# Two transformer layers on eight cores: the DMAs of the expert weights' preparation move from GpSimd's queue to SP's

## The chip, the cores and the metric

One Trainium2 chip, all 8 cores. Each core computes one of the 8 batch elements (2048 tokens of 1024 features), with no exchange between cores. The metric is the device time in microseconds of the slowest core.

## The reference

Layer 0 normalises x, and adds to x an attention (16 heads of 64, K also used as V) and a mixture of 8 experts. Layer 1 normalises again, and adds a causal attention with rotary embedding and a linear layer with ternary weights. The change lies in the experts of layer 0. Every expert is computed for every token; the two best by the router are weighted and summed:

```
g = softmax(h @ Wr); top2_w, top2_idx = top_k(g, 2); top2_w /= sum(top2_w)
hid = relu(einsum('bsh,ehf->bsef', h, W1))          # W1: 8 x 1024 x 4096
expert_out = einsum('bsef,efh->bseh', hid, W2)      # W2: 8 x 4096 x 1024
out = sum(take(expert_out, top2_idx) * top2_w)
```

## The kernel before

The kernel is written for five queues (TensorE, VectorE, ScalarE, GpSimd, SP). A small helper, `PB`, appends each operation to the list of its engine in the order of the Python code, and derives waits from the names (keys) that an operation reads and writes. An engine works through its list strictly in that order: an instruction that waits holds all behind it. `fence()` makes every key that is written for the first time afterwards wait for all semaphores as they stand at the fence, except for keys named as exempt.

The stages stand in this order in the code: `ln0`, `attn0`, `moe0`, `ln1`, `attn1`, `ffn1`.

`emit_attn0` loads its weights through the tile `stg` (two slots of 128 x 1024 fp32) with SP's queue and casts on VectorE. It ends with a fence that exempts `stg0`, `stg1`, `castb0` and `castb1`.

`emit_moe0` then has three parts.

1. SP loads `selb`, `idf32` and `wrstg`. The router runs over 16 tiles of 128 tokens (TensorE, VectorE, ScalarE).
2. The preparation (the loop at L686 to L730) turns the expert weights from fp32 into bf16 and lays them out for the loop, through scratch tensors `sw1` and `sw2` in HBM. For each of 8 experts it has 32 units for W1 and 32 for W2, 512 in all. A unit loads 512 KB into a slot of `stg`, casts it on GpSimd into a slot of `castb`, and stores 256 KB to `sw1` or `sw2`. A W1 load has contiguous runs of 2 KB, a W2 load of 512 B. Slots alternate. The store has `serialize=True`, so it also waits for the store before it on the same semaphore, two units earlier. All eight experts are written out here, ahead of part 3.
3. The expert loop goes over 8 experts and 4 blocks of 512 tokens, 32 passes. In a pass SP loads 8 blocks of 1 MB from `sw1` into `w1buf` (two slots; L755 multiplies, L763 applies ReLU into `hid`) and 8 blocks from `sw2` into `w2buf` (two slots; L776 multiplies, L784 and L788 weight and add to x). These loads read the keys `pp{ex}` and `ppB{ex}`, the last stores of that expert's preparation. A pass begins with the VectorE copy `cbs` (L740).

The helper's DMAs all carry L110 in the profile, or L134 where SP's waits are listed.

The lines that the change touches have this form, six of them:

```
pb.dma("gpsimd", stg[slot] <- w1_d[ex] ..., "pga"/"pgb", writes=[stg slot])
pb.op("gpsimd", castb[slot] <- stg[slot], reads=[stg slot], writes=[castb slot])
pb.dma("gpsimd", sw1_d[ex, fg] ... <- castb[slot], "ppw"/"ppw2", reads=[castb slot], serialize=True)
```

Of the kernel before, what the change touches and what calls it, by code (L numbers as in the profile page):

```python
# [150 lines left out]
def build_nc(stages=ALL_STAGES, dbg=None):  # L151
# [29 lines left out]
    with ExitStack() as ctx:  # L181
        pb = PB(nc, ctx)
# [424 lines left out]
        def emit_moe0(xn_done):  # L607
# [81 lines left out]
            for ex in range(NEXP):  # L689
                for fg in range(8):  # L690
                    for q in range(4):
                        slot = pti % 2
                        pti += 1
                        pb.dma("gpsimd",
                               stg[:, slot * 1024:(slot + 1) * 1024].rearrange(
                                   "p (c f) -> p c f", f=NT),
                               w1_d[ex].rearrange("(c p) (g f) -> g p c f",
                                                  p=128, f=NT)[fg][:, q * 2:(q + 1) * 2, :],
                               "pga" if slot == 0 else "pgb",
                               writes=[f"stg{slot}"])  # L700
                        pb.op("gpsimd", lambda e, slot=slot: e.tensor_copy(  # L701
                            castb[:, slot * 1024:(slot + 1) * 1024],
                            stg[:, slot * 1024:(slot + 1) * 1024]),
                            reads=[f"stg{slot}"], writes=[f"castb{slot}"])
                        pb.dma("gpsimd",
                               sw1_d[ex, fg, :, q * 1024:(q + 1) * 1024],
                               castb[:, slot * 1024:(slot + 1) * 1024],
                               "ppw" if slot == 0 else "ppw2",
                               reads=[f"castb{slot}"], serialize=True)
                for dc in range(8):  # L710
                    for qt in range(4):
                        slot = pti % 2
                        pti += 1
                        pb.dma("gpsimd",
                               stg[:, slot * 1024:(slot + 1) * 1024].rearrange(
                                   "p (fc j) -> p fc j", j=128),
                               w2_d[ex].rearrange("(fc p) (c j) -> c p fc j",
                                                  p=128, j=128)[dc][:, qt * 8:(qt + 1) * 8, :],
                               "pga" if slot == 0 else "pgb",
                               writes=[f"stg{slot}"])  # L720
                        pb.op("gpsimd", lambda e, slot=slot: e.tensor_copy(  # L721
                            castb[:, slot * 1024:(slot + 1) * 1024],
                            stg[:, slot * 1024:(slot + 1) * 1024]),
                            reads=[f"stg{slot}"], writes=[f"castb{slot}"])
                        pb.dma("gpsimd",
                               sw2_d[ex, dc, :, qt * 1024:(qt + 1) * 1024],
                               castb[:, slot * 1024:(slot + 1) * 1024],
                               "ppw" if slot == 0 else "ppw2",
                               reads=[f"castb{slot}"], serialize=True)
                pb._dep_update((), [f"pp{ex}"], ("ppw", pb.cnt["ppw"]))  # L730
                pb._dep_update((), [f"ppB{ex}"], ("ppw2", pb.cnt["ppw2"]))
# [540 lines left out]
        if "moe0" in stages:  # L1272
            emit_moe0(xn_done)
# [91 lines left out]
```

How the kernel before makes its waits and increments, by code:

```python
            def body(eng):  # L131
                for w, fn, incs in ops:
                    for s, c in w:
                        eng.wait_ge(sems[s], c)
                    ins = fn(eng)
                    for s, n in incs:
                        ins.then_inc(sems[s], n)
```

## Time and profile before

| | |
|---|---|
| median of the runs | 7590.35 us (7580.98 to 7599.72, 2 runs) |
| profiled execution | 6954.24 us, span of the slowest core 6952.5 us |
| spans of the eight cores | 6910.1 to 6952.5 us |
| mean granted TensorE clock | 0.878 to 0.881 |
| bytes moved by DMA, slowest core | 989.70 MB |

The profiled execution is shorter than the runs shown. Its rows are used for durations, and the sum of the prediction is made against its own time. A row of a group of instructions gives the line, the engine, the operation, output and input, and the count; "idle before" is how long the engine stood still just ahead of them, and what ended that. A row on DMA issues gives the median time from issue to landing. SPq is SP's queue.

### The profile page before, as it was taken

What the parts mean: (1) busy time and instruction counts of PE and PEld (TensorE: products, weight loads), DVE (VectorE), ACT (ScalarE), POOL (GpSimd) and SP (SyncE); (2) the same over time, 40 slices, a digit from 0 to 9 for tenths busy, and PEclk for the clock granted to TensorE, in tenths of its full rate; (3) what the DMA queues carried; (4) which work ended last, traced back from release to release, by engine and by line L of the source; (5) the groups of instructions that cost most, each with busy time, mean ns of one, the idle gap of its engine ahead of it and who ended that gap; (6) DMA issues with size and microseconds to landing.
All of it is one profiled execution on the core that took longest, in us unless ns stands there. A gap on an engine that the chain in (4) does not pass through costs nothing.

```text
span 6952.5 us, 84185 instructions; the slowest of 8 cores (6910.1 to 6952.5 us)
## 1 busy us (share of the span) xinstructions
PE 5330.6 (77%) x23271; PEld 2135.9 (31%) x23271; DVE 1426.1 (21%) x2644; ACT 1930.5 (28%) x2829; POOL 1247.7 (18%) x1553
## 2 busy tenths in 40 slices
PE   3666666656999999999999999999999335555536
PEld 0222222212444444444444444444444011111102
DVE  5222222222101010101010101001101633333336
ACT  0355555541111111111212111111111025545531
POOL 0233333332222222222222222220000000000000
PEclk9877777877999999999999999999999566767768
DMA  2434333335777777777777777775444000000011
GB/s 60 126 106 104 110 105 109 114 114 173 214 223 221 230 226 222 222 224 226 222 223 221 216 226 223 223 227 167 151 148 151 0 22 4 4 7 3 4 52 70
DMA packets 209081, 989.70 MB, mean 142 GB/s; under 512 B 27110, under 2 KB 37486, under 8 KB 141050
## 3 DMA queue, kind: packets, MB, share of 16 engines
q1 hardware_dynamic: 92794, 573.21, 25.3%
q0 software_dynamic: 115840, 411.11, 20.9%
q8 instruction: 210, 3.44, 0.2%
q14 instruction: 237, 1.94, 0.1%
HBM read 841.61 MB, written 142.61 MB: 142 GB/s over the span
## 4 chain that ended last, share of the span: by engine, by line
PE 57%; DMA 15%; ACT 11%; DVE 10%; issue 6%; DVEq 0%; ACTq 0%; SPq 0%; POOL 0%; POOLq 0%
PE bankA L776 20%; PE bankA L755 20%; DMA w1buf<-sw 7%; ACT exp L360 7%; DMA w2buf<-sw 6%; PE bankB L350 5%; PE bankA L338 2%; PE bank L493 2%; ACT rtmpB L927 1%; PE bankA L1132 1%; PE bankA L1233 1%; DVE rhl L450 1%; DVE rb L1083 1%; DVE rb L460 1%; DVE t1s L289 1%
## 5 line engine op out<-in xcount | busy, mean ns | idle before, releaser
L776 PE MATMUL bankA<-hid,w2buf 128*128 128x512 bf16 x8192 | 1793.0, 380 | 93.0 <-DMA w2buf<-sw 63.6
L755 PE MATMUL bankA<-xnTs,w1buf 128*128 128x512 bf16 x8192 | 1798.0, 381 | 69.7 <-DMA w1buf<-sw 69.2
L763 ACT ACTIVATE hid<-bankA 128x512 bf16<-128x512 f32 x1024 | 611.8, 598 | 3094.7 <-PE bankA L755 3094.7
L776 PEld LDWEIGHTS bankA<-hid,w2buf 128*128 128x128 bf16 x8192 | 794.8, 98 | 1091.3 <-issue 156.6
L755 PEld LDWEIGHTS bankA<-xnTs,w1buf 128*128 128x128 bf16 x8192 | 795.2, 98 | 1064.2 <-issue 133.1
L360 ACT ACTIVATE exp<-bankA,colpool 128x1024 bf16<-128x1024 f32 x832 | 908.1, 1114 | 493.9 <-PE bankA L338 459.6
L784 DVE TENSOR_TENSOR mtmp<-bankA,cbs 128x512 f32<-128x512 f32 x256 | 177.1, 692 | 3350.7 <-PE bankA L776 3350.7
L721 POOL CAST castb<-stg 128x1024 bf16<-128x1024 f32 x256 | 270.8, 1058 | 1502.0 <-DMA stg<-l0w 1502.0
L701 POOL CAST castb<-stg 128x1024 bf16<-128x1024 f32 x256 | 271.0, 1059 | 1488.4 <-DMA stg<-l0w 1488.4
L110 POOL DMA_DIRECT2D stg<-l0w x512 | 419.2, 819 | 229.8 <-DVE wkbf L310 204.4
L350 PE MATMUL bankB<-exp,vG 128*65 128x512 bf16 x640 | 258.8, 467 | 132.6 <-DVE exp L371 76.0
L110 POOL DMA_DIRECT2D sw<-castb x512 | 284.2, 555 | 279.0 <-POOL castb L721 139.6
L110 POOL DMA_DIRECT2D outT<-xTs x8 | 4.2, 536 | 1365.9 <-DVE xTs L1143 1365.6
L448 DVE CAST rhl<-rrow 1x512 bf16<-1x512 f32 x64 | 28.9, 451 | 882.4 <-ACT rrow L445 882.4
L788 DVE TENSOR_TENSOR xTs<-xTs,mtmp 128x512 f32<-128x512 f32 x256 | 188.0, 734 | 27.6 <-DVE mtmp L784 1.4
L452 PE MATMUL bankA<-rhl,onesb 1*128 1x512 bf16 x64 | 33.7, 527 | 181.6 <-DVE rhl L448 181.6
L371 DVE TENSOR_TENSOR exp<-exp,cmaskS 128x512 bf16<-128x512 bf16 x256 | 97.4, 422 | 337.7 <-ACT exp L360 337.7
L350 PE MATMUL bankB<-exp,vA0b 128*65 128x512 bf16 x256 | 110.7, 432 | 58.6 <-ACT exp L360 53.3
L350 PE MATMUL bankB<-exp,vA0a 128*65 128x512 bf16 x256 | 109.4, 427 | 58.6 <-ACT exp L360 53.3
L1075 PE MATMUL bank<-rhl,onesb 1*128 1x512 bf16 x64 | 35.7, 558 | 152.4 <-DVE rhl L1071 152.4
L338 PE MATMUL bankA<-qT,kT 64*128 64x512 bf16 x640 | 150.1, 465 | 0.1
L350 PEld LDWEIGHTS bankB<-exp,vG 128*65 128x65 bf16 x640 | 61.2, 119 | 282.2 <-issue 282.2
(218 smaller groups left out, 3167.4 us busy)
## 6 DMA issues: line engine op xcount, KB each, us to landing
stg<-l0w POOLq DMA_DIRECT2D x512, 512.0 KB, 5.7
w1buf<-sw SPq DMA_DIRECT2D x256, 1024.0 KB, 7.3
w2buf<-sw SPq DMA_DIRECT2D x256, 1024.0 KB, 7.1
sw<-castb POOLq DMA_DIRECT2D x512, 256.0 KB, 3.9
xTs<-xT SPq DMA_DIRECT2D x8, 1024.0 KB, 17.2
wtf<-l1wt SPq DMA_DIRECT2D x16, 512.0 KB
outT<-xTs POOLq DMA_DIRECT2D x8, 1024.0 KB, 11.6
stg<-l0wq SPq DMA_DIRECT2D x8, 512.0 KB, 4.5
```

The source lines that it names most:

```text
L110: self.on(qeng, lambda e, o=out, i=in_: e.dma_start(o, i), wait=w, inc=[(sem, 16)])
L338: lambda e, kc=kc, h12=h12, q4=q4, t=t: e.matmul(bank[q4][:, :], t["klhsT"](kc, h12), t["qrhs"][h12], start=True, stop=True),
L350: lambda e, kp=kp, h12=h12, q4=q4, t=t, nkc=nkc: e.matmul(bank[4 + h12][0:65, :], t["vap"](kp, h12), t["expb"][:, q4 * NT:(q4 + 1) * NT], ...
L360: lambda e, pp=pp, t=t: e.activation(t["expb"][:, pp * NT:(pp + 2) * NT], bankA[:, pp * NT:(pp + 2) * NT], AF.Exp, bias=t["negcol"]),
L493: e.matmul(bnk[:, :], wbf[:, dc * 1024 + hp * 128: dc * 1024 + (hp + 1) * 128], xnch(dc)[:, t0:t0 + NT], start=(dc == 0), stop=False),
L701: pb.op("gpsimd", lambda e, slot=slot: e.tensor_copy(castb[:, slot * 1024:(slot + 1) * 1024], stg[:, slot * 1024:(slot + 1) * 1024]), read ...
L721: pb.op("gpsimd", lambda e, slot=slot: e.tensor_copy(castb[:, slot * 1024:(slot + 1) * 1024], stg[:, slot * 1024:(slot + 1) * 1024]), read ...
L755: e.matmul(bnk[:, :], w1buf[:, slot * 4096 + dc * NT + fp * 128: slot * 4096 + dc * NT + (fp + 1) * 128], xnch(dc)[:, t0:t0 + NT], start=( ...
L763: pb.op("scalar", lambda e, f=f, bnk=bnk: e.activation(hid[:, f * NT:(f + 1) * NT], bnk[:, :], AF.Relu), reads=[bkkey], writes=[f"hid{f % ...
L776: e.matmul(bnk[:, :], w2buf[:, slot * 4096 + fc * 128:slot * 4096 + (fc + 1) * 128], hid[:, fc * NT:(fc + 1) * NT], start=(fc == 0), stop= ...
L784: pb.op("vector", lambda e, bnk=bnk, mslot=mslot: e.tensor_tensor(mtmp[:, mslot * NT:(mslot + 1) * NT], bnk[:, :], cbs[:], ALU.mult), read ...
L788: pb.op("vector", lambda e, dc=dc, t0=t0, mslot=mslot: e.tensor_tensor(xch(dc)[:, t0:t0 + NT], xch(dc)[:, t0:t0 + NT], mtmp[:, mslot * NT: ...
```

## The change

The queue of four DMA calls in the preparation is changed from `gpsimd` to `sync` (SP): the load and the store of the W1 units, and the load and the store of the W2 units. The casts, the tiles, the semaphores, their values, and the order of the code stay as they are. No function is new.

```
@@ preparation of W1, per unit @@
-                        pb.dma("gpsimd",
+                        pb.dma("sync",
                                stg[:, slot * 1024:(slot + 1) * 1024] ... <- w1_d[ex] ...
...
-                        pb.dma("gpsimd",
+                        pb.dma("sync",
                                sw1_d[ex, fg, :, q * 1024:(q + 1) * 1024],
                                castb[:, slot * 1024:(slot + 1) * 1024],
@@ preparation of W2, per unit @@
-                        pb.dma("gpsimd",
+                        pb.dma("sync",
                                stg[:, slot * 1024:(slot + 1) * 1024] ... <- w2_d[ex] ...
...
-                        pb.dma("gpsimd",
+                        pb.dma("sync",
                                sw2_d[ex, dc, :, qt * 1024:(qt + 1) * 1024],
                                castb[:, slot * 1024:(slot + 1) * 1024],
```

## Rows read from the trace of the kernel before

**Rows 1.** The page: busy time, share of the span and instructions of each engine.

```profile
PE 5330.6 (77%) x23271; PEld 2135.9 (31%) x23271; DVE 1426.1 (21%) x2644; ACT 1930.5 (28%) x2829; POOL 1247.7 (18%) x1553
```

**Rows 2.** Windows of core 0: length, busy us, granted clock, DMA share, GB/s.

```profile
2200.00:4600.00 2400.00, 2283.65 (x10407) 1007.78 (x10405) 246.50 (x348) 382.44 (x640) 593.45 (x738) 1.00 0.73 224
4800.00:5395.00 595.00, 589.42 (x2722) 265.31 (x2720) 64.92 (x96) 95.59 (x160) 0.00 (x0) 1.00 0.41 149
```

**Rows 3.** Tiles stg and sw, whole span: duration ns min/median/max, first and last start.

```profile
L110 POOL DMA_DIRECT2D stg<-l0w x512: 722/882/1133, 205.1 to 4729.1; - x171
...
L110 POOL DMA_DIRECT2D sw<-castb x512: 552/557/569, 211.0 to 4740.2; - x171
```

**Rows 4.** Waits of SP's queue: us in total, times, longest.

```profile
SPq L134 <- PE bankA L456: 1328.6, 1, 1328.6
...
SPq L134 <- DVE wqbf L315: 6.1, 8, 0.8
```

**Rows 5.** Timeline, 1527 to 1553 us: start, us, engine, line, operation.

```profile
1533.46 1.04 POOL L721 CAST castb<-stg 128x1024 bf16<-128x1024 f32 x1 [4.16 <-DMA stg<-l0w]
...
1535.05 0.55 POOL L110 DMA_DIRECT2D sw<-castb  x1 [0.54 <-POOL castb L721]
...
1542.64 0.69 DVE L471 TENSOR_TENSOR xTs<-xTs,t1s 64x512 f32<-64x512 f32 x1
...
1543.99 0.27 SPq L110 DMA_DIRECT2D selb<-sel  x1
1550.15 0.36 SPq L110 DMA_DIRECT2D idf<-idf32c  x1
...
1552.26 0.40 SPq L110 DMA_DIRECT2D wrstg<-l0wr  x1
...
1552.82 1.05 SPq L110 DMA_DIRECT2D w1buf<-sw  x2
```

**Rows 6.** DMA issues (KB, median us to landing); tiles stg; w1buf after 5100.

```profile
w1buf<-sw SPq DMA_DIRECT2D x256, 1024.0 KB, 7.3
w2buf<-sw SPq DMA_DIRECT2D x256, 1024.0 KB, 7.1
...
stg<-l0wq SPq DMA_DIRECT2D x8, 512.0 KB, 4.5
stg<-l0wk SPq DMA_DIRECT2D x8, 512.0 KB, 4.4
stg<-l1wq SPq DMA_DIRECT2D x8, 512.0 KB, 3.7
stg<-l1wo SPq DMA_DIRECT2D x8, 512.0 KB, 4.1
...
L110 SPq DMA_DIRECT2D stg<-l0wq x8: 327/328/426, 163.0 to 180.5; - x8
L315 DVE TENSOR_SCALAR wqbf<-stg x8: 693/694/695, 167.8 to 185.1; 128x1024 bf16<-128x1024 f32 x8
...
DMA to landing us min/median/max: 4.7/4.9/10.4
```

**Rows 7.** Preparation beside attention, W1 units 205 to 440 us, W2 units 440 to 672.

```profile
L110 POOL DMA_DIRECT2D stg<-l0w x33: 722/722/913, 205.1 to 434.6; - x33
L701 POOL CAST castb<-stg x32: 1030/1035/2272, 209.4 to 432.5; 128x1024 bf16<-128x1024 f32 x32
...
DMA to landing us min/median/max: 4.2/4.6/6.0
DMA to landing us min/median/max: 3.2/3.4/4.8
...
L110 POOL DMA_DIRECT2D stg<-l0w x30: 911/911/942, 442.3 to 668.5; - x30
...
DMA to landing us min/median/max: 4.8/5.4/6.2
DMA to landing us min/median/max: 2.9/3.7/5.0
```

**Rows 8.** Timeline of VectorE: first, later passes, and the expert loop's last addition.

```profile
1633.43 0.69 DVE L740 COPY cbs<-bankB 128x512 f32<-128x512 f32 x1 [1.97 <-PE bankB L736]
...
4719.07 0.69 DVE L740 COPY cbs<-bankB 128x512 f32<-128x512 f32 x1
4835.32 0.69 DVE L740 COPY cbs<-bankB 128x512 f32<-128x512 f32 x1
...
5284.19 0.68 DVE L740 COPY cbs<-bankB 128x512 f32<-128x512 f32 x1
...
5395.57 0.69 DVE L788 TENSOR_TENSOR xTs<-xTs,mtmp 128x512 f32<-128x512 f32 x1
```

More of the change, by code:

```diff
@@ L693, in emit_moe0 @@
                         pti += 1
-                        pb.dma("gpsimd",
+                        pb.dma("sync",
                                stg[:, slot * 1024:(slot + 1) * 1024].rearrange(
@@ L704, in emit_moe0 @@
                             reads=[f"stg{slot}"], writes=[f"castb{slot}"])
-                        pb.dma("gpsimd",
+                        pb.dma("sync",
                                sw1_d[ex, fg, :, q * 1024:(q + 1) * 1024],
@@ L713, in emit_moe0 @@
                         pti += 1
-                        pb.dma("gpsimd",
+                        pb.dma("sync",
                                stg[:, slot * 1024:(slot + 1) * 1024].rearrange(
@@ L724, in emit_moe0 @@
                             reads=[f"stg{slot}"], writes=[f"castb{slot}"])
-                        pb.dma("gpsimd",
+                        pb.dma("sync",
                                sw2_d[ex, dc, :, qt * 1024:(qt + 1) * 1024],
```

## The prediction

> **What bounds the kernel now.** I read the shares of the span first [rows 1], then the busy time by stretch [rows 2], then what each queue waited for [rows 3, 4], then single transfers in order of time [rows 5 to 7], and last the step of the expert loop [rows 8].
>
> The span has four stretches. Layer norm and loading of the attention weights run to 205 us. Attention of layer 0 follows; the last write of its result starts at 1542.64 and lasts 0.69 us, so it ends at 1543.3 [rows 5]. After the router, the experts run from 1633.4 to 5395.6, the start of their last addition [rows 8]. What comes behind takes 1557 us up to the span's end of 6952.5. In the experts TensorE is busy for 2283.65 us of 2400 (95%) at granted clock 1.00 while weights are also being prepared, and for 589.42 us of 595 (99%) once that is over [rows 2]. So TensorE bounds the expert stretch, and a small part is waiting for weights.
>
> The preparation is a second chain, wholly on GpSimd's queue: 512 units, each a load of 512 KB, a cast, and a store of 256 KB. It runs from 205.1 to 4740.2 plus the last store [rows 3], which is (4740.2 - 205.1)/512 = 8.86 us a unit. It is strictly serial, since a load is queued behind the store before it, and that store behind its cast. Today almost nobody waits for it: it has (1543 - 205)/7.2 = 186 units, nearly three experts' work, behind it when attention ends. The reader should see that GpSimd's busy share is only 18% [rows 1], and that this chain is all the same 4535 us long. It is hidden because it lies beside attention and beside the experts.
>
> **The change, part by part.** Three edits move all 1024 DMAs of the preparation (512 loads, 512 stores) from GpSimd's queue to SP's. The 512 casts stay on GpSimd. What counts is where they come to stand in SP's order. SP's queue at that point holds, in order: `selb`, `idf32` and `wrstg`, then (new) all 1024 DMAs for all eight experts, and then the 512 loads of `w1buf` and `w2buf` of the expert loop.
>
> *Ahead of them.* The load of `selb` is the first use of a new key behind the fence of the attention, so it waits for the attention's end. The trace has this as one wait of SP of 1328.6 us [rows 4], and the load goes at 1543.99 [rows 5]. On GpSimd's queue the preparation did not pass this fence (its keys are exempt) and started at 205.1. On SP's it stands behind `selb` and starts where the first `w1buf` load starts now, 1552.8 [rows 5]. The whole overlap with attention is gone.
>
> *Behind them.* The loads of `w1buf` for expert 0 need only the preparation of expert 0, but they are queued behind the preparation of expert 7. So TensorE, after the router (which ends near 1633 as now, and hides under the preparation), has nothing to do until all 512 units are through. The overlap with the experts is gone too. The preparation, at nothing today, now costs all it takes. Who waits behind: SP's loads, then TensorE on `w1buf`, then ScalarE and VectorE on TensorE, and layer 1 on them.
>
> *The unit on SP.* Its order stays serial: load, landing, cast, store issue, next load. The store does wait for the store two units before, which has long landed (median 3.4 to 3.7 us [rows 7]), and costs nothing.
> - Load, issue to landing. On SP no load of this preparation exists in the trace. Nearest are 512 KB loads of the same size into the same tile: `l1wq`, whose runs of 512 B have the shape of the w2 half, lands after 3.7 us, with nothing in front of it; `l0wq` and `l0wk` take 4.5 and 4.4 with the next load beside them, `l1wo` 4.1 [rows 6]. From GpSimd's queue, with the unit's own store just in front, it is 4.6 for w1 and 5.4 for w2 in the attention stretch, 0.72 and 0.91 of it the issue [rows 7], where SP's issue is 0.33 [rows 6]. Taking the difference in issue off gives 4.2 and 4.8. I take 4.5 for both; ends 3.7 and 5.2.
> - Cast 1.04 [rows 7].
> - Hops: SP waits 6.1 us in 8 times for casts by VectorE that last 0.69 [rows 4, 6], 0.76 each time, so a hop is below 0.1. Two hops and four waits for SP to work through: 0.2.
> - Store issue 0.33, as other loads and stores of 128 rows on SP [rows 6], and a gap of 0.04. On GpSimd this was 0.54 of idleness and 0.56 of issue behind each cast [rows 5, 7], so SP's path is some 0.7 us shorter.
>
> Sum 4.5 + 1.04 + 0.2 + 0.37 = 6.1 us. The ends are 3.7 + 1.61 = 5.3, and 7.2, which is GpSimd's own pace beside attention, (434.6 - 205.1)/32 [rows 7]. 8.86, its mean over everything, held only while 1 MB loads of the expert loop ran in the same engines; in the changed kernel they do not overlap at all, so I leave 8.86 to a rival.
>
> At this place the Trainium skill, page "DMA: Bandwidth & Descriptors", section "Specifications", gives about 1 us to the first byte from GpSimd's path and 0.6 from the hardware path. By it the unit would be 0.8 us shorter for its two transfers than GpSimd's 7.2, that is 6.4, and the preparation 154 us longer than by my value. The trace has no first byte to compare with.
>
> *What comes back.* Without the preparation's traffic, the loads of the expert loop land after 4.9 us instead of 7.3 and 7.1 [rows 6]. One pass (expert and 512 tokens) now takes (4719.07 - 1633.43)/26 = 118.7 us, and after the preparation's end (5284.19 - 4835.32)/4 = 112.2 [rows 8]. All 32 passes run at the second pace: 3590 us, where the stretch takes 3762 now. Gain 172 us. Attention loses its neighbour on the DMA engines; no row shows it waiting for a DMA, so nothing. If that is wrong it is a few tens of microseconds.
>
> **Sum, for the profiled execution.** 1552.8 (start of the preparation) + 512 x 6.1 = 3123 + 5 (first `w1buf` landing) + 3590 + 1557 (tail) = 9828 us, against 6954 now: +2874.
>
> The runs shown have a median of 7590, 636 above the profiled execution; no row shows where these lie. If they are a fixed amount, the changed kernel gets 636 as well; if a share of the time (9.15%), 900. A slower TensorE step in those runs would partly hide in the loop's waits for weights before and could not after, so I go between, 770. Predicted: 9828 + 770 = 10,600 us, some 40% slower.
>
> **Rivals.**
> - *The unit keeps its mean pace of 8.86.* For it: same bytes, same engines, and small runs of 512 B in the w2 half. Against it: beside attention it was 7.2, and the rise came only with the loop's loads. It would give 1552.8 + 4536 + 5 + 3590 + 1557 + 770 = 12,010.
> - *Loads run ahead.* The two slots of `stg` would allow a pace like that of the `l0wq` loads, (180.5 - 163.0)/7 = 2.5 us a load [rows 6], or about 3.8 with the stores' bytes: 9828 - 512 x 2.3 + 770 = 9420. Against it: the store of a unit stands ahead of the next load in SP's order and waits for the cast; it would need the order of a queue to be broken.
> - *The other side: no stall in front.* If the fence did not hold SP, and the loop's loads did not stand behind all the units, only the shorter unit would be left (8.86 less 1.1, as 7.2 becomes 6.1). The preparation would end near 205 + 512 x 7.8 = 4200 and the loop would gain at most the 172 us: 7590 - 172 = 7420, faster by 2.3%. The place is SP's queue at the first `w1buf` load, and the point from which it decides is whether that load goes near 1553 or after the last unit. Against it: the order in the code, and the wait of 1328.6 us [rows 4].
> - *Nothing to see.* Moving a DMA from one queue to another changes only its issue, 0.82 us and 0.56 us of GpSimd's time that nobody waits for: 7590. Against it: the same two reasons. The Trainium skill has this rule, "DMA: Bandwidth & Descriptors", section "Issuing engines are not separate DMA queues": where a DMA is issued saves only the sequencer's time. It speaks of bandwidth, and I follow it there (my landing times barely differ by queue); it says nothing of order.
>
> **How the numbers follow.** Forecast (unit between 5.3 and 7.2) 0.88; unit at 8.86 or near it 0.06; loads ahead 0.04; the other side 0.01; nothing to see 0.01. Every case but the last two is slower by far more than 2%, which is about what a measurement of this kernel can tell from no change: slower 0.98, same 0.01, faster 0.01. The range comes from the unit and the carrying over to the runs: low 9828 - 512 x 0.8 + 640 = 10,060; high 9828 + 512 x 1.1 + 900 = 11,290. The cases outside are the tails.
>
> **What would show it.** The first preparation load at about 1550 instead of 205. TensorE idle, and the DMA engines at about 768 KB in 6.1 us (some 130 GB/s), from about 1640 to 4680. GpSimd's casts 6.1 us apart, w1 and w2 halves nearly alike. The first `w1buf` load right behind the last store. Passes of 112 us, no waits for weights. Attention and layer 1 as long as now. I am wrong in kind if `w1buf` is loaded before the last unit or the preparation begins before 1540, and wrong in size mainly by the unit: 0.1 us in it is 51 us in the end.

## The result, and the profile after

The changed kernel is slower: 1.4186 times the kernel before (95% interval 1.4126 to 1.4245). It takes 9903 to 9915 us, its profiled execution 9914.8. The two runs of 7581 and 7600 us shown ahead of the prediction were disturbed ones; of the ten runs that the kernel before has by now, the five undisturbed ones took 6953 to 7022, near its profiled execution of 6954.

In microseconds this lies below the range of the prediction (10,060 to 11,290); the section on why the prediction was right, and where it was off, says which step put it there.

The page of the kernel before, busy tenths in 40 slices of its span:

```profile
PE   3666666656999999999999999999999335555536
...
POOL 0233333332222222222222222220000000000000
...
DMA  2434333335777777777777777775444000000011
```

The page of the changed kernel, shares of the span and the 40 slices (compare [rows 1]):

```profile
span 9912.7 us, 85699 instructions; the slowest of 8 cores (9841.1 to 9912.7 us)
...
PE 5305.8 (54%) x23271; PEld 2143.3 (22%) x23271; DVE 1404.8 (14%) x2644; ACT 1929.9 (19%) x2829; POOL 539.5 (5%) x529
...
PE   3766661000000000000799999999999998355554
...
POOL 0000001111111111111000000000000000000000
...
DMA  2000003444444444444444444444444442000002
```

TensorE's busy time is what it was, 5306 against 5331 us. What is new is a hole of twelve slices in its row, and GpSimd, which was busy from slice 2 to slice 27, is now busy in that hole and just ahead of it. In the attention, slices 2 to 6, the DMA engines now do nothing. This is the whole change at one look: a chain that lay beside two stages now stands between them.

The mean granted clock of TensorE fell from 0.878 to 0.755 on the slowest cores, which could look like a cause. It is not one: in the hole TensorE has no work, and in the expert loop it has the full clock, as before [rows 2]. Windows of core 7 (length, busy us of PE, PEld, DVE, ACT and POOL, granted clock, DMA share, GB/s):

```profile
1700.00:4700.00 3000.00, 0.00 (x0) 0.00 (x0) 0.00 (x0) 0.00 (x0) 497.64 (x479) 0.50 0.45 126
4800.00:8300.00 3500.00, 3467.64 (x16002) 1558.44 (x16000) 361.95 (x527) 599.97 (x1004) 0.00 (x0) 1.00 0.42 151
```

SP's queue around the fence, and around the end of the preparation (timeline: start, us, engine; compare [rows 5]):

```profile
1541.06 0.27 SPq L110 DMA_DIRECT2D selb<-sel  x1
1542.93 0.36 SPq L110 DMA_DIRECT2D idf<-idf32c  x1
1545.16 0.40 SPq L110 DMA_DIRECT2D wrstg<-l0wr  x1
1545.61 0.57 SPq L110 DMA_DIRECT2D stg<-l0w  x1
...
4745.92 0.37 SPq L110 DMA_DIRECT2D stg<-l0w  x1
4751.49 1.04 POOL L721 CAST castb<-stg 128x1024 bf16<-128x1024 f32 x1 [6.11 <-DMA stg<-l0w]
4752.62 0.34 SPq L110 DMA_DIRECT2D sw<-castb  x1
4753.01 0.91 SPq L110 DMA_DIRECT2D w1buf<-sw  x2
4761.28 4.00 PE L755 MATMUL bankA<-xnTs,w1buf 128*128 128x512 bf16 x9 [3135.28 <-DMA w1buf<-sw]
```

The first unit starts 0.45 us behind `wrstg`, the first load of `w1buf` 0.39 us behind the last store, and TensorE has waited 3135.28 us for it. The wait is put down to a DMA, but that DMA landed 8.1 us after it was issued at 4753.01. It was issued late, and the row that tells so is SP's.

What SP's queue waited for (us in total, times, longest; compare [rows 4]), and the DMA issues (KB, median us to landing; compare [rows 6]):

```profile
SPq L134 <- POOL castb L721: 1370.8, 256, 6.8
SPq L134 <- POOL castb L701: 1337.4, 256, 6.2
SPq L134 <- PE bankA L456: 1327.6, 1, 1327.6
...
stg<-l0w SPq DMA_DIRECT2D x512, 512.0 KB, 4.4
w1buf<-sw SPq DMA_DIRECT2D x256, 1024.0 KB, 4.9
w2buf<-sw SPq DMA_DIRECT2D x256, 1024.0 KB, 4.9
sw<-castb SPq DMA_DIRECT2D x512, 256.0 KB, 3.4
```

The one wait of 1327.6 us is the old one; it used to cost nothing. The 512 waits for casts, 2708 us, are new. SP waits there for the unit's own load and cast, and everything behind them in the queue waits too.

### The profile page after: what moved, and what is told of

It reads as the page before. It is cut to its first block, busy times and chain, and to the rows that moved or that the text cites. A ratio compares the mean times of both kernels' runs of the same rounds, so it can differ in the third digit from the quotient of the medians.

```text
span 9912.7 us, 85699 instructions; the slowest of 8 cores (9841.1 to 9912.7 us)
## 1 busy us (share of the span) xinstructions
PE 5305.8 (54%) x23271; PEld 2143.3 (22%) x23271; DVE 1404.8 (14%) x2644; ACT 1929.9 (19%) x2829; POOL 539.5 (5%) x529
## 2 busy tenths in 40 slices
DMA packets 504004, 989.78 MB, mean 100 GB/s; under 512 B 27110, under 2 KB 299630, under 8 KB 435962
## 4 chain that ended last, share of the span: by engine, by line
PE 46%; DMA 25%; ACT 7%; DVE 7%; POOL 5%; issue 5%; SPq 2%; POOLq 0%; DVEq 0%; ACTq 0%
DMA stg<-l0w 23%; PE bankA L755 17%; PE bankA L776 17%; ACT exp L360 4%; PE bankB L350 3%; POOL castb L701 3%; POOL castb L721 3%; SPq L110 2%; PE bankA L338 2%; PE bank L493 1%; ACT rtmpB L927 1%; PE bankA L1132 1%; PE bankA L1233 1%; DMA w1buf<-sw 1%; DVE rb L1083 0%
## 5 line engine op out<-in xcount | busy, mean ns | idle before, releaser
L755 PE MATMUL bankA<-xnTs,w1buf 128*128 128x512 bf16 x8192 | 1777.5, 379 | 3137.0 <-DMA w1buf<-sw 3137.0
L350 PE MATMUL bankB<-exp,vB0a 128*65 128x512 bf16 x256 | 111.0, 434 | 14.0 <-DVE t1s L467 14.0
L350 PE MATMUL bankB<-exp,vB0b 128*65 128x512 bf16 x256 | 108.2, 423 | 14.4 <-DVE t1s L467 14.4
```

The source lines that it names most:

```text
L350: lambda e, kp=kp, h12=h12, q4=q4, t=t, nkc=nkc: e.matmul(bank[4 + h12][0:65, :], t["vap"](kp, h12), t["expb"][:, q4 * NT:(q4 + 1) * NT], ...
L755: e.matmul(bnk[:, :], w1buf[:, slot * 4096 + dc * NT + fp * 128: slot * 4096 + dc * NT + (fp + 1) * 128], xnch(dc)[:, t0:t0 + NT], start=( ...
```

## The experiments

The theory: the transfers are as fast on SP as they were, and the loss is made of order alone. (1) The fence ahead of the preparation takes away the attention as a cover. (2) The expert loop's loads behind all 512 units take away the loop as a cover. (3) The store between a cast and the next load keeps the unit serial. Rivals: SP's queue or its transfers are slow in themselves, the DMA engines are the bound, or the loss grows with the number of DMAs moved. Every experiment computes the whole result. e1 to e5 have one profiled execution and no interval; they are compared by it, and the differences at stake are hundreds of us.

### e1: only the loads on SP

```
-                        pb.dma("gpsimd", stg[slot] <- w1_d / w2_d ...
+                        pb.dma("sync",   stg[slot] <- w1_d / w2_d ...
                         pb.dma("gpsimd", sw1_d / sw2_d <- castb[slot] ...     (as before)
```

> Change only half made: the 512 loads go on SP, the 512 stores stay on GpSimd. Theory (SP works strictly in order, and in the changed kernel each store stood between a cast and the next load): SP still starts behind the attention (first load near 1546 us) and the expert loop's loads still stand behind all 512 loads, but loads now run one unit ahead, so a unit takes 3.0 to 3.6 us; 1546 + 512 x 3.3 + 5 + 3593 + 1558 = 8390 us. Rival (a unit's time is the transfers' own, whatever the order): the unit stays at 6.3 us and the time at 9910.

Measured: 8662.6 us. The first load goes at 1531.7 us, behind the fence. The units take (3511.7 - 1531.7)/512 = 3.87 us, above the 3.0 to 3.6 that were forecast, so the time of 8390 was too short. The loop's first load goes at 3502.6, behind the last load of the preparation.

The timeline of GpSimd in this kernel tells the missing 0.57 us:

```profile
2001.54 1.04 POOL L721 CAST castb<-stg 128x1024 bf16<-128x1024 f32 x1 [1.05 <-DMA stg<-l0w]
...
2003.12 0.54 POOL L110 DMA_DIRECT2D sw<-castb  x1 [0.54 <-POOL castb L721]
2006.18 1.04 POOL L721 CAST castb<-stg 128x1024 bf16<-128x1024 f32 x1 [2.52 <-DMA sw<-castb]
```

The loads do run ahead, and now it is the cast that waits for a slot of `castb`, whose store of two units before lands only after a median of 5.7 us here. What ended the idle time ahead of the casts (us in total, times):

```profile
  DMA sw<-castb: 829.2, 354
```

With that, theory (3) holds: taking the stores out of SP's order makes a unit 2.4 us shorter, with the same bytes. The rival of a fixed unit falls. The forecast of the unit was too short because a second pair of slots became the limit.

### e2: only the stores on SP

```
                         pb.dma("gpsimd", stg[slot] <- w1_d / w2_d ...         (as before)
-                        pb.dma("gpsimd", sw1_d / sw2_d <- castb[slot] ...
+                        pb.dma("sync",   sw1_d / sw2_d <- castb[slot] ...
```

> The other half: loads and casts on GpSimd, stores on SP. Theory: GpSimd prepares two units near 205 us and then waits for slots of castb, because the first store stands behind the fence in SP's queue (about 1546 us). The loop's loads stand behind all stores. A unit is 0.72 to 0.91 issue, landing 4.6 to 5.4 with the issue, cast 1.04 and some 0.5 before the next issue: 6.6 us. 1546 + 510 x 6.6 + 5 + 3593 + 1558 = 10070 us, the slowest of all although half of the DMAs did not move. Rival (the loss grows with the number of DMAs that are moved to SP): half the loss, about 8430.

Measured: 9983.88 us (forecast 10,070), even slower than the full change. GpSimd's timeline shows the fence at work through another engine:

```profile
213.60 1.03 POOL L701 CAST castb<-stg 128x1024 bf16<-128x1024 f32 x1 [3.41 <-DMA stg<-l0w]
214.58 0.73 POOL L110 DMA_DIRECT2D stg<-l0w  x1
1532.71 1.03 POOL L701 CAST castb<-stg 128x1024 bf16<-128x1024 f32 x1 [1317.41 <-DMA sw<-castb]
```

Two units are cast, the third waits 1317.41 us for a store that stands in SP's queue behind `selb`. From there a unit takes (4827.9 - 1528.7)/510 = 6.47 us, where 6.6 was forecast. Half of the DMAs moved cost all of the loss, so it is not their number that counts.

### e3: the preparation written ahead of the fence

```
+            (the whole preparation loop, all on "sync")
             pb.dma("sync", selb[:, :], sel_d[:, :], "dmisc", writes=["selb"])
...
-            (the preparation loop, behind the router)
```

> The changed kernel with one move in the order of the code: the whole preparation is written ahead of the load of selb, so on SP it no longer stands behind the attention's end; the loop's loads (and the router's) still stand behind all 512 units. Theory: first unit near 205 us, 6.3 us a unit, end near 3430; then the three small loads and the router, 85 us, and the loop at 112 us a pass: 3430 + 85 + 3593 + 1558 = 8670 us. So the fence is worth about 1250 us of the loss of 2950 and the loop's loads behind the last unit the rest. Rival (the fence is harmless, the queue is slow in itself): no change from 9910.

Measured: 8795 and 8802 us on cores 2 and 3, at granted clocks of 0.782 and 0.784, and 8578 to 8651 on the other six, at 0.788 to 0.801; the forecast was 8670. I read core 5, the shortest, 8578.1; the same core took 9865.3 in the changed kernel and 6921.5 in the kernel before. Its rows (duration, first and last start), tiles `stg` and `cbs`:

```profile
L110 SPq DMA_DIRECT2D stg<-l0w x512: 378/379/1888, 207.6 to 3344.9; - x171
...
L740 DVE COPY cbs<-bankB x32: 681/684/690, 3431.3 to 6907.1; 128x512 f32<-128x512 f32 x32
```

On this core the preparation starts at 207.6 instead of 1526.2, and its last load goes 1338 us earlier (3344.9 instead of 4682.6). The time falls by only 1287, mainly because the router is no longer hidden: from the last load to the loop's first matmul it is 86 us instead of 13. A pass is (6907.1 - 3431.3)/31 = 112.1 us. Taking the fence away thus gives back 1287 of a loss of 2944 on this core, and 1261 to 1294 on each of the six cores. The remainder is the loop behind the last unit.

### e4: the loop's loads leave SP

```
-                        pb.dma("sync", w1buf[...] / w2buf[...] ...
+                        block_load(j + 2): pb.dma("scalar", w1buf[...] / w2buf[...] ...
                         (written behind the last matmul group of block j, whose slot it refills)
```

> The changed kernel with the expert loop's 512 loads of w1buf and w2buf issued from ScalarE's queue, each at the point of the order where its slot comes free; the preparation stays wholly on SP behind the fence. Theory: the loop no longer stands behind the preparation of all experts but behind that of its own. First pass at 1546 + 64 x 6.3 = 1950. From there the preparation, with the loop's traffic beside it, takes 7 to 8.3 us a unit, 64 units 450 to 530 us against 4 passes of 118 = 472: the two run about level. End of the preparation near 1950 + 448 x 7.6 = 5350, then the last expert, 449, and the tail 1558: 7360 us (7100 to 7600). Rival (moving the preparation to SP makes the transfers themselves slow, or the DMA engines are the bound): stays above 9000.

Measured: 7677.99 us, above the range of 7100 to 7600, and 2237 us less than the changed kernel. The loop's first matmul starts at 1935.4. Its waits for weights (us in total, times, longest):

```profile
PE bankA L767 <- DMA w1buf<-sw: 796.0, 72, 328.1
...
PE bankA L786 <- DMA w2buf<-sw: 73.5, 69, 3.0
```

The 328.1 is the wait for the first expert. Most of the rest falls at the changes of expert: a pass there takes 2596.65 - 2410.65 = 186 us against 117 within an expert. The preparation beside the loop took (5659.0 - 1925.7)/448 = 8.33 us a unit, 533 us an expert, from the last store of expert 0 to that of expert 7, and four passes of the loop need only some 470; I had reckoned with 7.6. So the loop follows the preparation throughout. The fence is untouched here, and the serial unit too; what was taken away is the place of the loop's loads behind all 512 units.

The gains of e3 and e4 do not add up to the loss: 1287 and 2237 are 3524, and the loss is 2960. Each was measured with the other stall in place. Once the loop waits only for its own expert, the fence costs it 64 units and not 512: its first matmul starts at 1935.4, some 300 us later than in the kernel before.

### e5: the stores one unit later in SP's order

```
-            load(i); cast(i); store(i)
+            load(i); cast(i); store(i - 1)
```

> The changed kernel with all DMAs on SP and the preparation at the same place, but each unit's store written behind the next unit's load (load i, store i-1), so that SP never holds a load back for a cast. Theory: first load near 1540 us, the unit goes from 6.26 to about 3.4 us (in the half change with stores on GpSimd it was 3.87, where the next cast waited for a store of 5.7 us; SP's stores land in 3.4), total 1540 + 512 x 3.4 + 9 + 3593 + 1558 = 8440 us (8340 to 8690). Rival (the transfers of one queue do not overlap usefully): 9900.

Measured: 8530.65 us in its profiled execution, within the 8340 to 8690 that were forecast. A unit takes (3377.5 - 1529.7)/512 = 3.61 us. All DMAs are on SP and the fence and the loop's place are as in the changed kernel; only the order inside the preparation differs, and 1384 us are gone. The median landing of a load is 5.3 us and of a store 3.9, both longer than in the serial unit (4.4 and 3.4); here a load and a store are under way together. The core moved 218 GB/s between 1700 and 3300 us, where the changed kernel moved 126 in its hole, so the DMA engines were not what bound the serial preparation.

### e6: nothing left behind the preparation

```
             (e3 and e4 together)
-            pb.dma("sync",   selb / idf32 / wrstg ...
+            pb.dma("scalar", selb / idf32 / wrstg ...
```

> The changed kernel with both stalls taken away and the serial unit kept: the preparation written ahead of the fence (as in e3), and the router's three loads and the expert loop's loads issued from ScalarE's queue (as in e4). Theory: nothing stands behind the preparation any more; it starts near 205 us, has 212 units behind it when the attention ends, and the remaining 300 at 8.3 us end near 4030, always ahead of the loop. Attention, router, loop and tail as in the kernel before, with 21 instead of 27 passes at 118.7 us and the rest at 112.2: 6915 us against 6953 before (6880 to 6990), so the queue itself costs nothing. Rival (part of the loss is in the hardware queue's transfers or in their contention with the loop): above 7200.

Measured: 0.9938 (0.9912 to 0.9965) of the kernel before, profiled execution 6903.73 us. All 1024 DMAs of the preparation are on SP in the serial form of the changed kernel. The loop runs from 1629.1.

```profile
L110 SPq DMA_DIRECT2D stg<-l0w x512: 378/384/2148, 206.7 to 4066.4; - x171
```

The last unit's load goes at 4066.4 (forecast 4030). In the same surroundings, attention and then loop, GpSimd's queue took from 205.1 to 4729.1 for the same loads [rows 3]. So the whole loss is gone, and SP's queue is not slow in itself: it is through 660 us sooner.

### e8: the control for e4 and e6

```
             (the kernel before; only the loop's loads as in e4)
```

> Control: the kernel before with only the expert loop's loads issued from ScalarE's queue, the preparation on GpSimd. Theory: the queue of the loop's loads is worth nothing, 6953 us within 0.5%. If it comes out slower, that amount is in e4 and e6 too and has to be taken off there.

Measured: 1.0024 (0.9977 to 1.0072). Whether SP or ScalarE issues the loop's loads is worth nothing that these runs can tell. The last load of its preparation, on GpSimd, goes at 4708.3, against 4066.4 in e6.

### e7, e10 and e11: all on SP, in the order of need

```
+            for i in range(384): unit_step(i)          # load(i), store(i-1); ahead of selb. 336 in e10, e11
             pb.dma("sync", selb ...
...
             pb.dma("sync", w1buf / w2buf ...            # block k of the loop
+            unit_step(384 + k)                          # while there are units left
```

> All DMAs on SP as in the changed kernel, put in the order in which they are needed: units pipelined (load i, store i-1), the first 384 written ahead of the fence, the last 128 one beside each block of the expert loop's first 8 passes. Theory: 384 units at 3.4 us fill the attention stretch (205 + 1310 = 1515); the loop starts near 1630; 8 passes with traffic beside them at about 120, 24 at 112.2; tail 1558: 1630 + 960 + 2693 + 1558 = 6840 us, against 6953 before (faster by 1.0 to 2.0%). If a unit in attention takes 3.9 us, the loop starts some 160 us later and the time is about 7000. Rival (any preparation on SP costs the loop): above 7100.

Measured: 0.9949 (0.9917 to 0.998), half a per cent faster, where 1 to 2% had been expected. In SP's timeline of this kernel the three small loads came too late:

```profile
1668.91 0.30 SPq L110 DMA_DIRECT2D selb<-sel  x1
1670.93 0.35 SPq L110 DMA_DIRECT2D idf<-idf32c  x1
1672.83 0.38 SPq L110 DMA_DIRECT2D wrstg<-l0wr  x1
1673.55 0.33 SPq L110 DMA_DIRECT2D w1buf<-sw  x1
```

A unit beside the attention took (1668.9 - 206.9)/384 = 3.8 us instead of 3.4, the units ahead of the fence overran the attention, and the router started some 125 us late. That is the stall of the changed kernel in small.

> As e7, with 336 units ahead of the fence instead of 384. In e7 a unit beside attention took 3.75 us and the loop started 125 us late. Theory: 336 x 3.75 = 1260, so the units ahead end near 1465, before the attention does, and the loop starts near 1630 as in the kernel before; 11 passes at 118, 21 at 112.2, tail 1558: 1630 + 1298 + 2356 + 1558 = 6842 us, and no more than 6870: some 1.3 to 1.8% under the kernel before (e7: 0.5%). Rival (e7's late start was not what it lost, but the clock or the DMA engines): no better than e7, 6900 or more.

Measured: 6849.13 us in its profiled execution (forecast 6842), without an interval; e11 is the same kernel. The last store ahead of the fence and what follows:

```profile
1399.90 0.37 SPq L110 DMA_DIRECT2D stg<-l0w  x1
1402.61 0.34 SPq L110 DMA_DIRECT2D sw<-castb  x1
1544.75 0.30 SPq L110 DMA_DIRECT2D selb<-sel  x1
...
1549.41 0.38 SPq L110 DMA_DIRECT2D stg<-l0w  x1
1549.94 3.01 SPq L110 DMA_DIRECT2D sw<-castb  x1
1553.01 1.40 SPq L110 DMA_DIRECT2D w1buf<-sw  x1
```

SP now waits for the attention's end with all due work done. The loop starts at 1631.2; its first 11 passes take (2933.81 - 1631.2)/11 = 118.4 us, later ones 112.0.

> The kernel of e10 once more, because only two of its eight runs were undisturbed and so its comparison had no interval. Theory as there: 6842 us, 0.980 to 0.986 of the kernel before. Rival: those two runs were lucky, 0.99 or above.

Measured: 0.9846 (0.9812 to 0.9879). This is the fastest version. Its gain over the kernel before is the passes without traffic beside them: 21 of 32, where it was 5.

## Why the prediction was right, and where it was off

In direction, mechanism and size of the loss it was right: the sum for the profiled execution was 9828 us, 2874 more than before, and the span is 9912.7, 2960 more. In the time that it named, 10,600 us, it was not: the runs took 9903 to 9915, below the low end of its range. By its own terms:

| term | predicted | measured |
|---|---|---|
| first unit | 1552.8 | 1545.6 |
| 512 units | 3123 (6.10 each) | 3207 (6.26 each) |
| to the first matmul | 5 | 8.7 |
| 32 passes | 3590 (112.2) | 3593 (112.2) |
| tail | 1557 | 1558 |

**The place in SP's order.** Right, and shown from both sides: e3 takes the fence away, e4 the loop's place, e6 both. The rivals "the other side" and "nothing to see" would have needed a preparation that starts near 205 us; its first load went at 1545.61. e6 is what the first of them would have looked like. It gave 0.9938, where 7420/7590 = 0.978 was worked out: that took the full 172 us of the loop, but some 21 passes still had the traffic beside them.

**The unit.** 6.26 instead of 6.10, 84 us in all. The transfer was right: over the 512 units the mean from a load's issue to its landing is 4.46 us, where 4.5 was put. The terms that were too small are the small ones. From the landing to the start of the cast it is 0.24, where a hop of 0.1 was put; from the store's issue to the next load's 0.44, where 0.37 was. The cast's end to the store's issue is 0.08. The hop of 0.1 had been read from SP waiting for VectorE; GpSimd waiting for a DMA is another wait, and none of the rows showed it. W1 units took (1742.0 - 1550.4)/31 = 6.18, W2 units (1946.4 - 1748.6)/31 = 6.38: alike, as forecast. Loads of the changed kernel from 1700 to 3200 us, and the timeline of two casts:

```profile
DMA to landing us min/median/max: 3.7/4.4/6.0
...
1556.92 1.04 POOL L701 CAST castb<-stg 128x1024 bf16<-128x1024 f32 x1 [5.47 <-DMA stg<-l0w]
1562.86 1.04 POOL L701 CAST castb<-stg 128x1024 bf16<-128x1024 f32 x1 [4.89 <-DMA stg<-l0w]
```

The estimate that followed from the Trainium skill, page "DMA: Bandwidth & Descriptors", section "Specifications", was 6.4, and my own 6.1; the measured 6.26 lies halfway, and does not decide between them.

**The first matmul.** 8.7 us instead of 5. The first two loads of `w1buf`, of 1 MB each, go 0.47 us apart and right behind the last store, and the first lands after 8.1 us, not after the median of 4.9.

**The rival of 8.86 us a unit.** Rightly set aside for the changed kernel, where nothing runs beside the preparation. But it shows what the loop's traffic does to a unit: e4, with the same order in the unit and the loop beside it, came to 8.33.

**What comes back.** Passes of 112.2 us, median landing of the loop's loads 4.9 us: right. The gain of 172 us is there; without it the loss would have been larger still.

**Attention and layer 1.** As long as before: the attention's end moved by 3 us, the tail by 1.

**The carrying over to the runs.** This step failed. I added 770 us, between a fixed amount and a share, since the median shown lay 636 us above the profiled execution. The changed kernel's time is level with its profiled execution, and so is that of the kernel before. The right amount was 0, and the right sentence would have been 9828. The 636 us belonged to those two runs, not to the kernel, and no row of the trace spoke for them. Even the low end of the range had 640 us of it, so the time came out below the range. That the ratio is near all the same, 10,600/7590 = 1.397 against 1.4186, is luck: the 770 above the line and the 636 below it nearly cancel. The profiled sums alone give 9828/6954 = 1.413, inside the interval.

**A slip.** The prediction speaks of three edits; the diff has four, and the counts of 512 loads and 512 stores go with four.

**In the experiments** the forecasts failed where a resource that had been slack became the limit: `castb`'s two slots in e1, the preparation's own pace beside the loop in e4, and a unit of 3.8 instead of 3.4 us in e7. What a unit costs when it is no longer serial was not settled further: e5 gives 3.61 alone, e1 3.87 with stores on GpSimd, e7 3.8 and e10 (1402.6 - 211.5)/335 = 3.56 beside the attention.

## What to carry to other kernels

Before moving a DMA to another queue, write down what stands ahead of it and behind it there, fences included, and ask for each how long it waits; the transfers themselves took no longer here, and the whole loss was order. A long serial chain that costs nothing is free only by its place: 4535 us of preparation were hidden, and 3135 of its 3207 us lay bare once its queue was shared with the loop's loads. If one queue must do both, order its work by when it is needed and put each store behind the next load; that turned a loss of 42% into a gain of 1.5%.

## What the runs showed of the hardware

**A load of 512 KB lands nearly alike from either queue.** 4.4 us from SP in the changed kernel, 4.6 (W1) and 5.4 (W2) from GpSimd beside the attention [rows 7], and 5.3 from GpSimd in e2, where only the preparation was under way. These times hold the issue, 0.38 us on SP and 0.72 to 0.91 on GpSimd; without it 4.0 stands against 3.9 to 4.5. The Trainium skill says that DMAs of different issuing engines run on the same 16 engines and interleave ("DMA: Bandwidth & Descriptors", section "Issuing engines are not separate DMA queues"); these landings agree, and so does e8's 1.0024 for SP and ScalarE; which engines carried a transfer, no row here shows.

**Smaller packets cost little or nothing here.** The page of the kernel before and of the changed one:

```profile
DMA packets 209081, 989.70 MB, mean 142 GB/s; under 512 B 27110, under 2 KB 37486, under 8 KB 141050
...
DMA packets 504004, 989.78 MB, mean 100 GB/s; under 512 B 27110, under 2 KB 299630, under 8 KB 435962
```

The same bytes go in 2.4 times as many packets. The difference under 2 KB is 299630 - 37486 = 262144 = 256 x 1024, the 512 B runs of the W2 loads, which were recorded as larger packets when GpSimd issued them. e1 (loads on SP) has the 299630 too, e2 (loads on GpSimd) the 37486. Still the W2 units are only 0.2 us longer than the W1 units. In e2, with the larger packets, W2 loads land later than W1 loads as well, by 0.3 us (5.4 against 5.1).

**A store from GpSimd landed later beside SP's loads.** Its median was 5.7 us in e1, where SP's loads ran one ahead, against 3.4 to 3.7 in the serial unit [rows 7]; SP's own store in the same order (e5) took 3.9. Whether the queue or its place among the loads makes the difference was not tried apart.

**A cast starts 0.24 us after its load has landed.** This is the mean over the 512 units of the changed kernel; in the kernel before it was 0.19.
